# Sums of weights turned by DMA instead of TensorE, and the order of the last block shifted

## What is computed

```python
local_scores = jnp.where(adj_matrix, lQ @ lK.T * scale, -1e9)
max_score = max(max(local_scores, axis=1), global_scores, es)
le, ge, ee = (jnp.exp(s - max_score) for s in (local_scores, global_scores, es))
denom = jnp.sum(le, axis=-1, keepdims=True) + ge + ee
res = le / denom @ lV + ge / denom * gV + ee / denom * eV
x = x + jnp.maximum(res, masked_x)
...
x_attn = normed @ attn_w.T + attn_b + xf          # normed: layer norm of xf
h = gelu(einsum('meti,ehi->meth', tok, fc1_w) + fc1_b)
y = einsum('meth,edh->metd', h, fc2_w) + fc2_b
x = x + gelu(y @ next_w.T + next_b)
```

## Time and profile before

| | |
|---|---|
| runs (us) | 1114.56, 1114.46, 1113.06; median 1114.46 |
| the profiled execution's own time | 1113.44 |
| its span in the trace | 1111.6 |
| mean granted clock of PE | 0.983 |
| PE busy | 1058.7 (95%) |
| DVE busy | 855.8 (77%) |
| POOL busy | 713.7 (64%) |
| ACT busy | 558.1 (50%) |
| DMA | 187.70 MB, mean 169 GB/s |

### The profile page before, as it was taken

The page is one execution under the profiler, slowest core; times in us unless marked ns, Lnnn a source line. Parts: engine busy times, 40 slices in busy tenths (PEclk is TensorE's granted clock), DMA queues, the critical chain, the costliest instruction groups (busy, mean ns, idle before and its releaser), DMA issues.

```text
span 1111.6 us, 15940 instructions
## 1 busy us (share of the span) xinstructions
PE 1058.7 (95%) x5060; PEld 882.6 (79%) x5060; DVE 855.8 (77%) x1523; ACT 558.1 (50%) x994; POOL 713.7 (64%) x713
## 2 busy tenths in 40 slices
PE   6877899999999999999999999998898999999997
PEld 4755688888888888888888888877786888888886
DVE  5768988788888878878979878887885775577642
ACT  5544144444444445444444444456666466755573
POOL 5656586687777777768768677677583455554550
PEclk8998999999999999999999999998999999999998
DMA  8694543443453444444435434359735636654421
GB/s 269 206 336 144 186 133 125 141 161 129 156 166 124 147 165 143 139 146 158 151 133 171 137 128 162 128 182 349 265 122 187 229 122 238 228 190 163 160 76 57
DMA packets 102086, 187.70 MB, mean 169 GB/s; under 512 B 10226, under 2 KB 41843, under 8 KB 101747
## 3 DMA queue, kind: packets, MB, share of 16 engines
q1 hardware_dynamic: 102002, 186.69, 49.4%
HBM read 147.29 MB, written 30.98 MB: 160 GB/s over the span
## 4 chain that ended last, share of the span: by engine, by line
PE 81%; DVE 7%; issue 4%; ACT 3%; DMA 3%; POOL 2%; SPq 1%; DVEq 0%; ACTq 0%; POOLq 0%
PE u_ps L1488 20%; PE s_ps L52 11%; PE s_ps L54 11%; PE s_ps L53 11%; PE u_ps L1495 10%; PE u_ps L54 2%; PE u_ps L52 2%; PE u_ps L53 2%; DMA v_scratch<-vst 1%; PE mb_ps L52 1%; PE mb_ps L54 1%; PE mb_ps L53 1%; PE s_ps L1552 1%; PE mt_ps L53 1%; PE mt_ps L52 1%
## 5 line engine op out<-in xcount | busy, mean ns | idle before, releaser
L681 POOL TENSOR_TENSOR p_lo<-p_all,p_hi 128x512 fp32r<-128x512 f32 x224 | 295.0, 1317 | 158.2 <-PE u_ps L1495 94.8
L1228 ACT ACTIVATE p_hi<-scores 128x512 fp32r<-128x512 f32 x224 | 141.6, 632 | 337.4 <-DVE scores L841 337.2
L855 DVE TENSOR_TENSOR scores<-s_ps,bias 128x512 f32<-128x512 f32 x256 | 175.8, 687 | 96.3 <-PE s_ps L54 85.0
L1488 PE MATMUL u_ps<-p_hi,v_in 128*128 128x512 f32 x896 | 241.0, 391 | 0.0
L52 PE MATMUL s_ps<-q_hi,lnT_hi 128*128 128x512 f32 x512 | 203.4, 397 | 10.4 <-DVE scores L855 8.4
L54 PE MATMUL s_ps<-q_hi,lnT_lo 128*128 128x512 f32 x512 | 201.1, 393 | 0.0
L53 PE MATMUL s_ps<-q_lo,lnT_hi 128*128 128x512 f32 x512 | 201.1, 393 | 0.0
L1488 PEld LDWEIGHTS u_ps<-p_hi,v_in 128*128 128x128 f32 x896 | 167.2, 188 | 34.0
L673 POOL TENSOR_SCALAR bias<-adj 128x512 f32<-128x512 uint8 x256 | 164.5, 644 | 13.1 <-DVE scores L855 13.1
L841 DVE TENSOR_TENSOR scores<-scores,mb_ps 128x512 f32<-128x512 f32 x256 | 171.8, 677 | 0.8 <-PE mb_ps L1514 0.8
L869 DVE TENSOR_TENSOR kept_ps<-kept_ps,scores 128x512 f32<-128x512 f32 x232 | 162.3, 699 | 8.0
(11 more groups left out here) (207 smaller groups left out, 1814.2 us busy)
## 6 DMA issues: line engine op xcount, KB each, us to landing
v_in<-v_scratch SPq DMA_DIRECT2D x118, 512.0 KB, 3.7
adj<-in_adj SPq DMA_DIRECT2D x64, 256.0 KB, 3.8
raw<-in_wffn SPq DMA_DIRECT2D x32, 512.0 KB, 4.9
v_scratch<-vst SPq DMA_DIRECT2D x8, 1024.0 KB, 5.9
mx<-in_mx SPq DMA_DIRECT2D x18, 256.0 KB, 6.9
xg<-in_x SPq DMA_DIRECT2D x8, 512.0 KB, 5.8
mg_raw<-in_mxT SPq DMA_DIRECT2D x16, 256.0 KB, 4.1
uhi_scratch<-uT_high SPq DMA_DIRECT2D x8, 512.0 KB, 2.7
```

The source lines that it names most:

```text
L681: nc.gpsimd.tensor_tensor(out=low_part(y), in0=whole_part(y), in1=high_part(y).bitcast(fp32), op=ALU.subtract).then_inc(plo_ready, 1)
L855: nc.vector.tensor_tensor(scores[:, t % SLOTS], s_ps[t % 3][:, :], bias[:, t % 2], ALU.add).then_inc(masked, 1)
L1228: nc.scalar.activation(high_part(y), scores[:, y % SLOTS], ACT.Exp, scale=SCALE).then_inc(phi_ready, 1)
L1488: nc.tensor.matmul(u_ps[d][:, :], values[:, x % 2, at:at + P], high_part(x), start=k == 0 and part == 0, stop=False)
```

## The change

The sums no longer go over PE. SP stores row 0 of uT (2 KB in one partition) to DRAM when the block has ended, and two steps later loads it back as a column per 128 queries into a new small buffer, sums. shares reads that instead of PSUM, and all that follows lies two steps later: shares at 6 steps after the block's end, u's store at 5, the coefficients' at 8, kt's at 22 (block 6 at 29), scaled_rows at 16, extra_rows at 19, which is k = 24 (block 6 as before). POOL takes low_result's second half first, one step after the block's end, and the first half three steps after it, when the row has been stored. PE no longer waits for earlier denominators in turn_tops.

In the final block the ring of exponentials' buffers gets a written order, exponentials start one further ahead two steps earlier, DVE's low parts are made one step later, and all steps beside the weighing from i = 15 on lie one step later. In expert 0, shares lies at j = 3 instead of 2, scaled_rows at 4 instead of 6, extra_rows in two pairs at j = 5 and 6 instead of four at 7, and the second normalisation (of expert 1's rows) at j = 0 and 1 instead of 1 and 2.

```diff
+        sums = rings("sums", [P, 2, TG])
...
+        LATE_SLOTS = (2, 0, 3, 5, 4, 1, 6)
...
-            return p_hi[:, y % 3] if y < LAST else p_late[:, (y - LAST) % LATE]
+            return p_hi[:, y % 3] if y < LAST else p_late[:, LATE_SLOTS[(y - LAST) % LATE]]
+
+        def late_slot_free(j):
+            return LAST + max(j + 1 - LATE, (-2, -1, -1, -1, 0, 0, 0)[j % LATE])
...
-            return 2 if i < 0 else min(LATE - 2, 3 + i // 2)
+            return 2 if i < -2 else min(LATE - 2, 3 + (i + 2) // 2)
...
+                def store_sums(n):
+                    sp.wait_ge(u0_copied, n + 1)
+                    sp.dma_start(sum_dram[n:n + 1], uT[0:1, 0, :]).then_inc(row_stored, 16)
+
+                def load_sums(n):
+
+                    sp.wait_ge(row_stored, 16 * n + 16)
+                    wait(sp, den_ready, n - 1)
+                    sp.dma_start(sums[:, n % 2], sum_dram[n].rearrange("(t p) -> p t", p=P), allow_slow_non_contiguous=True).then_inc(sums_loaded, 16)
...
-                    ended = ended_since(t, 3, 13)
+                    ended = ends_block(t)
+                    if ended is not None:
+                        store_sums(ended)
+                    ended = ends_block(t - 2)
+                    if ended is not None:
+                        load_sums(ended)
+                    ended = ended_since(t, 5, 13)
...
-                    pool.wait_ge(sum_done, n + 1)
+                    if k == 0:
+                        pool.wait_ge(row_stored, 16 * n + 16)
...
-                    dve.wait_ge(sum_done, n + 1)
-                    nc.vector.tensor_tensor(den, sum_bank(n)[:, 0:TG], extra_sum, ALU.add).then_inc(den_ready, 1)
+                    dve.wait_ge(sums_loaded, 16 * n + 16)
+                    nc.vector.tensor_tensor(den, sums[:, n % 2], extra_sum, ALU.add).then_inc(den_ready, 1)
...
-                        if e == 0 and j == 2:
+                        if e == 0 and j == 3:
                             shares(BLOCKS - 1)
-                        if e == 0 and j == 7:
-                            extra_rows(BLOCKS - 1)
+                        if e == 0 and j in (5, 6):
+                            extra_rows(BLOCKS - 1, range(2 * j - 10, 2 * j - 8))
...
-                            if j == 1:
+                            if j == (1 if n > 1 else 0):
                                 normalise(n, 0)
...
-                    for y in exponentials_in(t - 1):
+                    for y in exponentials_in(t - 2):
...
-                    wait(act, pv_done, y - 2 if y < LAST else max(y + 1 - LATE, min(y - 1, LAST)))
+                    wait(act, pv_done, y - 2 if y < LAST else late_slot_free(y - LAST))
+                    if y in (LAST + 2, LAST + 4):
+                        act.wait_ge(plo_ready, LAST - 1 + (y - LAST - 2) // 2)
...
-                    wait(pe, den_ready, n - 1)
...
-                    if i == 15:
+                    if i == 16:
                         turn_normed(0, 0)
                         turn_first(0, 0)
...
-                        if e == 0 and j == 1:
-                            add_up(BLOCKS - 1)
...
-                    ended = ends_block(t)
-                    if ended is not None:
-                        add_up(ended)
```

More of the change, by code:

```diff
@@ L272, in gnn_moe_kernel @@
             sem(n) for n in ("u0_copied", "u1_copied", "uhigh_ready", "ulow_ready", "u_stored"))
[L273 to L274 removed]
+        row_stored, sums_loaded, gsum_ready, den_ready, coef_ready, coef_stored = (
+            sem(n) for n in ("row_stored", "sums_loaded", "gsum_ready", "den_ready", "coef_ready", "coef_stored"))
         STEPS = TILES + LAG
@@ L607, in _ @@
                 sp.dma_start(b2_c[:, :], b2).then_inc(b_loaded, 16)
-                for t in range(KT, STEPS + 8):
+                for t in range(KT, STEPS + 9):
                     n, k = divmod(t, KT)
@@ L931, in low, with extra_rows @@
                     nc.vector.tensor_tensor(out, whole, high.bitcast(fp32), ALU.subtract).then_inc(done, 1)
-                def extra_rows(n):
-                    for tt in range(TG):
+                def extra_rows(n, tiles):
+                    for tt in tiles:
                         dve.wait_ge(ktg_ready, 4 * n + tt + 1)
@@ L1203, in _ @@
                             top_extra(n)
-                    ended = ends_block(t - 4)
+                    ended = ends_block(t - 6)
                     if ended is not None:
                         shares(ended)
-                    ended = ended_since(t, 17, 25)
+                    ended = ended_since(t, 19, 25)
                     if ended is not None:
-                        extra_rows(ended)
+                        extra_rows(ended, range(TG))
                     beside(t - LAG - LAST)
@@ L1345, in expert @@
                             high_weights(e, HB - WLEFT + j)
+                        if e == 0 and j == 4:
+                            scaled_rows(BLOCKS - 1)
                         if n < E:
@@ L1363, in expert @@
                             high_masked(n + 1)
-                        if e == 0 and j == 6:
-                            scaled_rows(BLOCKS - 1)
                     for k in range(KD):
@@ L1515, in spread_tops @@
                     last.then_inc(spread_done, 1)
-                def add_up(n):
-                    pe.wait_ge(u0_copied, n + 1)
-                    pe.wait_ge(top_ready, min(n + 2, BLOCKS))
-                    for j in range(TG):
-                        last = nc.tensor.matmul(sum_bank(n)[:, j:j + 1], uT[0:1, 0, j * P:(j + 1) * P], ident[0:1, 0:1], start=True, stop=True)
-                    last.then_inc(sum_done, 1)
                 def parts(hi, lo, index, what):
```

59 lines of the change are left out of this document (29 added, 30 removed).

## The result

The changed kernel took 1097.58 us (median of 4 runs, 1096.27 to 1097.99), the kernel before 1114.51 (1113.06 to 1114.63): a ratio of 0.9843, with a 95% interval of 0.9824 to 0.9862. The prediction was 1097.5, in a range of 1090 to 1106.

What follows compares the result with a forecast made beforehand. The prediction took TensorE to bound the blocks, with single waits from the final block into the experts. Gains 5.5 + 4.2 + 3.4 + 3.4 = 16.5 from 1113.44 gave 1096.9, plus 0.6 for the median: 1097.5 us, range 1090 to 1106.

Steps and rivals of the forecast that it cites:

- The blocks: Six blocks: L1522 off TensorE saves 6 x 1.20 = 7.2 us, less 1.7 for shares: 5.5 (1.5 to 7.2).
- The 1.7 for shares at k = 11: Six blocks: shares at its later place makes TensorE wait 0.28 us per block, from 0 to 0.95.
- the first rival: Six blocks: VectorE late through shares or the four rows, TensorE waits about 1.0 per block; about 1102 us; chance 0.20.
- extra_rows at k = 24: Six blocks: the four rows, moved from k = 22, take r about 1.7 us where GpSimd is idle; cost 0.
- The third rival: Six blocks: the four rows at k = 24 take 6.02, TensorE waits 4.0 per block; 1121 us; chance 0.05.
- The final block: Final block: 1.8 for L1522, 0.3 for uT, 1.4 for xn, 0.8 clock, less 0.1: 4.2 us (1 to 6).
- The low clock behind the wait for uT: Final block: 0.57 over 752 to 760 us, priced at 3.4; only 0.3 of the uT wait counted as saved.
- The 2.2 for xn: Final block: normalise's result used one step later, 1.4 us less wait for xn, plus 0.8 of lost clock.
- The step for res: Final block: with sums stored and loaded back, the 2.0 us wait for res becomes 1.1 to 3.4, taken as 2.1.
- the second rival: Final block: sums come late, wait for res 3.4 or more with lower clock, gain near 0; 1101.7 us; chance 0.14.
- Expert 0: Expert 0: moved scaled_rows and split extra_rows remove waits, 2.9; earlier normalise 0.5: 3.4 us (1 to 4.7).
- Expert 1: Expert 1: earlier kt and x_mid stores remove the 2.1 nT_lo wait and 1.7 of clock: 3.4 us (0 to 3.8).

Runs made afterwards that it cites:

- e2_shares_back: Changed kernel with shares back at four steps after the block's end (k = 9), sums still by transfer: median 1101.03 us.
- first pair: The first traces of the kernel before and of the changed kernel; medians 1114.51 and 1097.58 us.
- e6_ring_back: Changed kernel with the order of the final block's exponentials put back (buffers, ahead, VectorE's low parts one step sooner): median 1103.77 us.
- e3_beside_back: Changed kernel with the steps beside the last block's weighing from i = 15 on put back one step sooner: median 1099.01 us.
- e4_expert_back: Changed kernel with expert 0 as before (shares, scaled_rows, extra_rows and second normalisation at their old places): median 1103.36 us.
- e5_kt_late: Changed kernel with SP storing kt of block 7 only when the low part of xT for expert 1 is made: median 1101.05 us.
- second pair: The kernel before and the changed kernel, both unedited, traced once more on another chip; medians of runs 1115.48 and 1101.09 us.
- after_again: The changed kernel itself, unedited, for a second trace on another chip: median 1101.09 us, ratio 0.9863 to the kernel before there.
- e9_last_by_pe: Changed kernel with block 6's sums turned by TensorE again and shares of blocks 0 to 5 at k = 9: median 1096.05 us, ratio 0.9823.

## Why the prediction was right, point by point

**The blocks.** Forecast 5.5, measured 5.9. The 1.20 per block was right to the hundredth, and 7.2 is what e2_shares_back has (584.20 - 577.00). The 1.7 for shares at k = 11 was 1.3, 0.50 in two of the blocks, 0.22 in a third and nearly nothing in the others. It came by the mechanism of the first rival at the smaller price. The prediction took the low end because a whole subtraction would have to lie in the way, and that reason failed: the addition was held for 1.23 to 1.28 in five of the six blocks (0.16 in PSUM). But a centre 0.57 later lost mostly to the margin, so the size was right by luck. For extra_rows at k = 24 the choice of r = 1.7 by the idle time of GpSimd was right, in all six blocks. On DVE:

```profile
281.93 1.66 DVE L960 SCALAR_TENSOR_TENSOR kt_out<-bev_b,coefs,kt_out 128x256 f32<-128x256 f32 x4
```

The third rival, 6.02 for the same rows, didn't come. The load of the sums was costed too dear: the bounds were 3.6 to 14.4, the loads landed after a median of 2.5, below the lower bound. In the DMA issues by kind (count, KB each, us to landing):

```profile
sums<-sum_scratch SPq DMA_DIRECT2D x8, 2.0 KB, 2.5
```

**The final block.** Forecast 4.2, measured 5.1 in the first pair of traces, but by other parts, of which two were mis-sized. The low clock behind the wait for uT was taken as staying; it went with the exponentials' new order, which made that wait 0.3 shorter (e6_ring_back shows that order to be the cause), so the first four weighings gained 4.3 instead of 1.8. The 2.2 for xn (wait and clock) was 0.3, which is within scatter (e3_beside_back): its wait shrank, and later ones grew. The step for res was right as a risk and wrong as a size: 0.3 in one trace, 2.8 in the other. There the final block gained 3.0, and the prediction's own sign of the second rival was seen: a wait for res over 2 us, and shares waiting for the sums. On that chip the changed kernel took 1101.09 against 1115.18 (the median of all 13 runs of the kernel before there), near the rival's 1101.7. But the low clock that the rival adds didn't come, and its reason, transfers that land late, counts only as far as it puts the addition behind GpSimd's subtraction. With the load kept, 2.7 to 3.2 is the usual wait: six of the seven traces have it, and the first one is the exception. Which of the runs without a trace had it is not known.

**Expert 0.** Forecast 3.4, measured 3.7, and e4_expert_back gives the 3.7 back. scaled_rows and extra_rows now lie where the prediction put them, ScalarE's in 1.70 and VectorE's in two pairs:

```profile
833.32 1.70 ACT L1299 ACTIVATE kt_out<-gv_b,coefs 128x256 f32<-128x256 f32 x4
```

```profile
838.68 0.87 DVE L960 SCALAR_TENSOR_TENSOR kt_out<-bev_b,coefs,kt_out 128x256 f32<-128x256 f32 x2
...
841.40 1.92 DVE L960 SCALAR_TENSOR_TENSOR kt_out<-bev_b,coefs,kt_out 128x256 f32<-128x256 f32 x2
```

The normalise one part sooner wasn't free, as it was taken to be: its four instructions run beside GpSimd at 821.69 to 826.09, 1.83 and 2.65 for pairs, and the low part behind them comes late, which is the new wait of 1.9 for h_lo. What it saved later, waits of 0.67 for xf and 1.12 for nT_lo, about made up for it; e4_expert_back puts all of expert 0 back at once and doesn't part the two.

**Expert 1.** Forecast 3.4 with 3.8 as the upper end, measured 4.3. The chain from kt to x_mid to nT_lo is shown by e5_kt_late. The size depends on whether the clock falls: 1.4 and 2.5 where it stayed (e4, e5), 4.3 and 5.3 against the two traces of before, where it fell.

**What the sum left out.** 4.3 us ahead of step 40 in the first pair, against the change; none of the steps concerned that part. So the sum of the four terms, 16.5, met a median difference of 16.9, while the traces show 19.0 gained in the four stretches and 4.3 lost at the start. Right in its four signs, the forecast owes some of its closeness to errors that cancel: the clock (2.5 too little) against xn (1.9 too much) and the start. On the chip of the second pair the medians, 1101.09 and 1115.18, differ by 14.1.

## What to carry to other kernels

Take small work off the engine that bounds a stage, but look at what reads the result: an operand moved from PSUM to SBUF can put VectorE behind GpSimd, and 0.1 us of order then decides over 2 us. Send results by DMA where the queue is quiet and a block's time is left (577.0 in the blocks), and not where they are needed within a few steps among the weights of the last stage; e9_last_by_pe does each where it fits. Price a shorter wait together with the clock behind it, and expect part of a saving in a tight stretch to come back as the next wait.

## What the runs showed of the hardware that I had not expected

A load that scatters 512 single numbers landed in 2.5 us, sooner than the store of the coefficients in 128 pieces had in the kernel before (3.6); in the changed kernel, two steps later in the block, that store took 2.1 itself. In the final block, while weights moved, the load of the sums took 6.1. A VectorE addition of 128x4 with both inputs in SBUF ended 0.02 to 0.03 us behind the GpSimd subtraction that it began beside in four traces, after 0.19, 0.73, 0.76 and 1.21 us. The granted clock kept at 1.00 after a wait of 1.46 and fell to the lower level (0.57 over the stretch) after one of 1.78 at the same place, each time. But the length of the wait alone doesn't tell: at the wait for res it fell behind 2.73 (e5_kt_late, 0.50 over 768.00 to 771.40) and not behind 2.75 (after_again, 1.00 over the same stretch), and in expert 1 it stayed after 2.08. In the traces with the new buffer, used or not, the first 40 steps took 1.2 to 4.3 us longer than in the two without; whether that is the places in memory or scatter is not settled.
